# Finer groups of routing weights, exponents from one difference and two Relu, four more split units, and steps placed anew

## The reference, cut to what matters

```
x = x + attention(layernorm(x))                 # 8 sequences, 512 x 128
x = x + experts(layernorm(x))                   # first layer of experts
x = x + rwkv(layernorm(x))                      # time mixing, channel mixing
x = x + experts(layernorm(x))                   # second layer of experts

experts(x):                                     # 32 experts of width 64, top 4 of a softmax
    y = sum_e  w_e * ((silu(x @ W1[e]) * (x @ W3[e])) @ W2[e])
    z = (silu(x @ Ws1) * (x @ Ws3)) @ Ws2       # shared expert, width 128

wkv(w, u, k, v), for each token t, with carry aa, bb, pp:
    ww = u + k;   qq = max(pp, ww);   e1 = exp(pp - qq);   e2 = exp(ww - qq)
    y  = (e1 * aa + e2 * v) / (e1 * bb + e2)
    ww2 = pp + w; qq2 = max(ww2, k);  e1b = exp(ww2 - qq2); e2b = exp(k - qq2)
    aa, bb, pp = e1b * aa + e2b * v,  e1b * bb + e2b,  qq2
```

## Time and profile before

| | before |
|---|---|
| device time, median of 3 runs | 793.45 us |
| lowest and highest of the runs | 793.45 and 793.64 us |
| span of the profiled execution | 791.7 us |
| busy: PE / DVE / ACT / POOL | 99 / 82 / 72 / 79% of the span |
| DMA, mean over the span | 102 GB/s, 80.7 MB |

### The profile page before, as it was taken

One profiled execution on the slowest core, in us unless ns is written; L12 is line 12 of the kernel. 1 busy time (PEld: TensorE's weight loads), 2 busy tenths in 40 slices (PEclk: granted clock), 3 DMA queues, 4 the chain that ended last, 5 costly groups with the idle time before them and its releaser, 6 DMA issues.

```text
span 791.7 us, 12780 instructions
## 1 busy us (share of the span) xinstructions
PE 785.1 (99%) x3817; PEld 596.4 (75%) x3817; DVE 645.9 (82%) x1539; ACT 567.9 (72%) x1055; POOL 625.3 (79%) x491
## 2 busy tenths in 40 slices
PE   8999999999999999999999999999999999999998
PEld 5777778676776777768778777887778767788786
DVE  6875577997997989998988869988689889767686
ACT  5677787868768778689765867668685775677553
POOL 6687779849767797769987888998797877876985
PEclk9999999999999999999999999999999999999999
DMA  9353334243144342462425444253444424425552
GB/s 326 95 123 82 87 92 113 66 102 92 42 113 113 73 105 54 110 133 58 120 60 134 104 93 107 65 143 79 110 113 95 90 68 110 111 59 115 124 127 74
DMA packets 49332, 80.73 MB, mean 102 GB/s; under 512 B 3280, under 2 KB 14544, under 8 KB 48880
## 3 DMA queue, kind: packets, MB, share of 16 engines
q1 hardware_dynamic: 48976, 79.72, 42.1%
q10 hardware_dynamic: 288, 0.20, 0.1%
HBM read 75.19 MB, written 4.72 MB: 101 GB/s over the span
## 4 chain that ended last, share of the span: by engine, by line
PE 51%; POOL 2%; issue 2%; DVE 1%; ACT 0%; DVEq 0%; POOLq 0%; ACTq 0%
PE pa L1039 5%; PE pb L1039 4%; PE py L1067 4%; PE pa L1043 4%; PE pb L1043 4%; PE pa L1040 4%; PE pb L1040 4%; PE pu L1326 4%; PE py L1072 3%; PE py L1074 3%; PE py L1073 3%; POOL m_h L587 1%; PE pq L1283 1%; PE pu L1310 1%; PE pv L1334 1%
## 5 line engine op out<-in xcount | busy, mean ns | idle before, releaser
L587 POOL TENSOR_TENSOR m_h<-m_v,m_wb 128x512 f32<-128x512 f32 x254 | 364.3, 1444 | 98.7 <-DVE m_v L1468 42.9
L732 ACT ACTIVATE m_th<-pa 128x512 f32<-128x512 f32 x220 | 130.6, 594 | 102.0 <-PE pa L1043 97.7
L1468 DVE TENSOR_TENSOR m_v<-m_th,pb 128x512 f32<-128x512 f32 x205 | 138.6, 679 | 23.9 <-ACT m_th L732 15.5
L1039 PE MATMUL pa<-m_xh,w1h 128*128 128x512 f32 x272 | 137.2, 504 | 0.3 <-DVE m_v L1471 0.2
L416 DVE TENSOR_TENSOR m_hl<-m_h,m_hh 128x512 fp32r<-128x512 f32 x120 | 111.4, 929 | 24.8 <-ACT m_hh L921 24.1
L921 ACT ACTIVATE m_hh<-m_h 128x512 fp32r<-128x512 f32 x184 | 115.2, 626 | 13.8 <-POOL m_h L587 13.1
L1039 PE MATMUL pb<-m_xh,w3h 128*128 128x512 f32 x272 | 115.4, 424 | 0.0
L1043 PE MATMUL pa<-m_xl,w1h 128*128 128x512 f32 x272 | 107.3, 394 | 0.3 <-POOL m_xl L608 0.3
L1043 PE MATMUL pb<-m_xl,w3h 128*128 128x512 f32 x272 | 107.1, 394 | 0.0
L1040 PE MATMUL pa<-m_xh,w1l 128*128 128x512 f32 x272 | 106.6, 392 | 0.0
L1040 PE MATMUL pb<-m_xh,w3l 128*128 128x512 f32 x272 | 106.5, 391 | 0.0
(11 more groups left out here) (318 smaller groups left out, 1653.8 us busy)
## 6 DMA issues: line engine op xcount, KB each, us to landing
m_wb<-w_scratch SPq DMA_DIRECT2D x126, 512.0 KB, 6.5
x_sb<-in_x SPq DMA_DIRECT2D x8, 256.0 KB, 7.2
m_wb<-in_w SPq DMA_DIRECT2D x2, 1024.0 KB, 6.8
x_out<-x_sb SPq DMA_DIRECT2D x7, 256.0 KB, 6.6
u_scratch<-t_u SPq DMA_DIRECT2D x6, 256.0 KB, 2.6
t_u<-u_scratch SPq DMA_DIRECT2D x6, 256.0 KB, 2.7
f_kk<-in_w SPq DMA_DIRECT2D x1, 1024.0 KB, 9.7
w_scratch<-r_wT SPq DMA_DIRECT2D x16, 64.0 KB, 1.5
```

Of the source, the lines that this page charges most:

```text
L587: pool.tensor_tensor(hidden(g, p), gated(g, p), m_wb[:, p % (GRING * GP), :], ALU.mult).then_inc(sig["m_h"], 1)
L732: ins = act.activation(m_th[:, p % 2, :], pa[p % 2][:, :], ACT.Silu)
L1039: pe.matmul(ps[:, :], high[:, p, :], xh, start=True, stop=False)
L1468: dve.tensor_tensor(gated(g, p), m_th[:, r, :], pb[r][:, :], ALU.mult).then_inc(sig["m_v"], 1)
```

## The change

**Groups.** GROUPS goes from 4 to 8 and GRING from 2 to 4: a group is now two units, a load half as large, and a place of two units is loaded again as soon as these two are through. In pass 0 the first group is not loaded at all. The saved sequences' transfers (keep) are issued ahead of group 4 instead of group 2, that is, ahead of unit 8 in both.

**Time mixing.** `t_qq` on DVE and both differences on POOL go. DVE forms one difference for each pair, and ACT makes two Relu from it and then the Exp of the negative: four ACT instructions of 128 by 512 more for each sequence.

**Units.** Four units go from native to split (pass 0 unit 9, pass 1 unit 11, pass 4 unit 7, pass 13 unit 3), four more form `m_th` by Tanh (52 to 56), and the tables LOW_ON_POOL and LOW_LATE change: of the 188 rests 125 are on DVE and 63 on POOL, of the 184 before 120 and 64.

**Slots.** Nearly every table of slots has new numbers, on all five engines; the work in the steps is otherwise the same.

```diff
-GROUPS = 4
+GROUPS = 8
-GRING = 2
+GRING = 4
 NATIVE = (
-    (3, 9),
-    (11,),
+    (3,),
+    (),
...
+        def weights_in(g, j):
+            return 32 * (GROUPS // GRING * g + j // GRING + (0 if j % GRING == 0 else 1))
...
-                for j in range(GROUPS):
+                for j in range(1 if q == 0 else 0, GROUPS):
...
-                    first = SPREAD if q == 0 and j == 0 else 0
                     for h in range(2):
-                        sp.dma_start(m_wb[H * h:H * (h + 1), at + first:at + GP, :],
-                                     w_scratch[q, j, first:GP, h, :].partition_broadcast(H)).then_inc(wb_in[j], 16)
+                        sp.dma_start(m_wb[H * h:H * (h + 1), at:at + GP, :],
+                                     w_scratch[q, j, :, h, :].partition_broadcast(H)).then_inc(wb_in[j % GRING], 16)
...
-                if p % GP == 0 or (g == 0 and p == SPREAD):
-                    pool.wait_ge(wb_in[p // GP], 32 * g + 32)
+                if p % GP == 0:
+                    pool.wait_ge(wb_in[p // GP % GRING], weights_in(g, p // GP))
...
-                if slot == (26, 24, 24, 23, 25, 30, 32, 25)[m]:
-                    pool.wait_ge(sig["t_pp"], m + 1)
-                    pool.tensor_tensor(t_ea[:, 1, :], t_k[:, :], t_pp[:, 1:1 + S], ALU.subtract).then_inc(sig["t_a1"], 1)
-                if slot == (29, 29, 28, 29, 43, 32, 33, 30)[m]:
-                    pool.wait_ge(sig["t_qq"], m + 1)
-                    pool.tensor_tensor(t_eb[:, 0, :], t_pp[:, 0:S], maxima(m), ALU.subtract).then_inc(sig["t_b0"], 1)
...
                     act.wait_ge(sig["t_a0"], m + 1)
-                    act.wait_ge(sig["t_a1"], m + 1)
-                    act.activation(wide(t_ea[:, :, :]), wide(t_ea[:, :, :]), ACT.Exp).then_inc(sig["t_expa"], 1)
+                    act.activation(t_ea[:, 1, :], t_ea[:, 0, :], ACT.Relu).then_inc(sig["t_ra"], 1)
+                if slot == (29, 33, 33, 34, 38, 37, 33, 32)[m]:
+                    act.wait_ge(sig["t_ra"], 2 * m + 1)
+                    act.activation(t_ea[:, 0, :], t_ea[:, 0, :], ACT.Relu, scale=-1.0).then_inc(sig["t_ra"], 1)
...
+                if slot == (33, 35, 33, 34, 41, 38, 36, 32)[m]:
+                    act.wait_ge(sig["t_ra"], 2 * m + 2)
+                    act.activation(wide(t_ea[:, :, :]), wide(t_ea[:, :, :]), ACT.Exp, scale=-1.0).then_inc(sig["t_expa"], 1)
...
-                    dve.scalar_tensor_tensor(out=maxima(m), in0=t_k[:, :], scalar=vec[:, FIRST:FIRST + 1],
-                                             in1=t_pp[:, 0:S], op0=ALU.add, op1=ALU.max).then_inc(sig["t_qq"], 1)
-                if slot == (27, 29, 28, 29, 34, 39, 32, 29)[m]:
+                if slot == (27, 29, 28, 26, 35, 35, 26, 27)[m]:
                     dve.scalar_tensor_tensor(out=t_ea[:, 0, :], in0=t_pp[:, 0:S], scalar=decay[:, 0:1],
-                                             in1=t_pp[:, 1:1 + S], op0=ALU.add, op1=ALU.subtract).then_inc(sig["t_a0"], 1)
+                                             in1=t_k[:, :], op0=ALU.add, op1=ALU.subtract).then_inc(sig["t_a0"], 1)
...
```

371 lines of the change are left out of this document (186 added, 185 removed), and 4 rows, old and new, of the table NATIVE.

## The result

The changed kernel takes 795.69 us, the median of 20 runs (793.97 to 798.14), against 793.13 us of the kernel before (20 runs, 792.52 to 794.13): 2.6 us slower, and by the ratio of the runs 1.0029, 95% interval [1.0023, 1.0035]. The forecast was 793.8 us.

What follows compares the result with a forecast made beforehand. The prediction took TensorE, busy 99% of the span, to bound the kernel. From 793.45 us it added 1.8 for the start and took off 0.64 for split units and 0.8 for new places: 793.8 us, range 791.0 to 796.4.

Steps and rivals of the forecast that it cites:

- The start: Start of the kernel: sequence 1's statistics wait for its transfer, delaying row maxima and the router's transposes; +1.8 us, bounds 0 and 2.4.
- rival C: TensorE's clock falls in the new gap at the start, 1.6 us extra, 795.4 us; chance 0.10.
- Four split units: Four units turned from native to split save TensorE 0.16 us each, -0.64 us; what they add elsewhere costs nothing.
- TensorE's steps placed anew: TensorE's order: changes from small to fp32r matmuls fall from 156 to 147, 0.09 us each, -0.8 us.
- Time mixing and groups: Exponents by Relu on ScalarE and half-sized weight loads: both off TensorE's path, costed at nothing.
- the half pass between the exponents and their use: Time mixing: the cover that keeps its added ScalarE work free; without it, 0.63 us at each Relu ahead of a Silu.
- the forecast's case: Whole kernel: the forecast of 793.8 us, some 793.0 to 794.7; chance 0.42.
- slower: Whole kernel: a time above 795.04 us, told apart from no change by about 0.2%; chance 0.25.

## Why the prediction was right or wrong

**The start** (+1.8 us forecast). The mechanism is right step by step, up to the tenth. Its size was 1.7 us against the execution profiled before, and is nearer 1.2 against others, since the earlier trace rows come from an execution whose matmuls went at the full rate early. The term was taken from one execution, and that moment moves the old start by 0.2 to 1.0 us from trace to trace, which the bounds of 0 and 2.4 cover but the working doesn't name. What I had not seen is that two causes give the same end: with the maxima early again, GpSimd's order and a root stretched by 0.9 us hold `r_q` at 21.87.

**The clock** (rival C, given 0.10). By the granted clock of the executions it happens in 11 of 20, and costs 1.9 us where it does (796.34 - 794.41; 1.6 forecast). What was wrong is the weight: I argued that fillings on both sides protect the gap, and with the same fillings around it the clock fell in 11 of 20. With the gap filled it fell in none of 11. Its length alone doesn't decide either: with transposes at 15.40 behind an idle 2.28 us it fell in four of five (statistics ahead of everything), and behind an idle 2.33 us it stayed up in the profiled execution of the native units. What does decide is open. That C's 795.4 is so near the measured median is in part luck: it stands on a sum of 793.8, and the executions without the fall have 794.4.

**Four split units** (-0.64 us). Right for TensorE's work, 0.7 us. The statement that what they add costs nothing elsewhere is right only in the new order, where taking them back costs 0.8 to 1.0 us; alone in the old one they bring waits of about 1.8 us.

**TensorE's steps placed anew** (-0.8 us). Wrong, and wrong as a reading of the profile. I took the 0.32 us between the first and the second fp32r matmul behind small ones for 0.09 us of a price per change of kind. Look at the small matmul ahead of it instead, in the trace of the kernel before:

```profile
99.80 0.27 PE L1224 MATMUL pq<-ident,r_p 128*128 128x128 f32 x1
99.83 0.48 PE L1039 MATMUL pa<-m_xh,w1h 128*128 128x512 f32 x1
100.15 0.40 PE L1040 MATMUL pa<-m_xh,w1l 128*128 128x512 f32 x1
```

The small product starts at 99.80 and the next matmul 0.03 us behind it, though a small one takes TensorE 0.11 us (the three transposes from 309.85 to the next row at 310.18 take 0.33). The 0.09 us behind it are the small one's own time, which shows one interval late: from the fp32r matmul ahead (99.57) to the second one behind (100.15) are 0.58 us, and without a small one between them it is twice 0.23, 0.46 us; the difference is 0.12 us, the small one's own time. Fewer changes of kind don't remove it.

What the new places do instead isn't settled. I add up over each order the usual start-to-start time of each matmul, the median over all traces of the same matmul in the same surroundings, from the first L1039 of pass 0 to the last of pass 15. With one neighbour on each side as the surroundings this gives 753.8 us both before and after, with two ahead and one behind 754.6 and 753.7. The split units alone give 0.7 less in either count. So the new places lie between a cost of 0.6 us and a gain of 0.3 us of work; the 0.8 us are not in either.

**The middle as a whole.** From the first to the last of these matmuls (24.17 to 783.17 before, 25.88 to 784.26 after; the first of after stands above). Before:

```profile
24.17 0.48 PE L1039 MATMUL pa<-m_xh,w1h 128*128 128x512 f32 x1
```

```profile
783.17 0.40 PE L1039 MATMUL pb<-m_xh,w3h 128*128 128x512 f32 x1
```

After:

```profile
784.26 0.39 PE L1042 MATMUL pb<-m_xh,w3h 128*128 128x512 f32 x1
```

The stretch takes 759.0 us before and 758.4 after. But two experiments whose middle is that of the kernel before take 757.9 and 758.4, and five with the middle of the change 758.1 to 758.6. So on the mean the middle has gained 0.1 us, not the forecast 1.4, and the traces of the old order alone are 1.1 us apart. Since the split units do give 0.7, the rest of the middle has lost about as much. Which part of it did is open: no run has the tanh units, the tables LOW_ON_POOL and LOW_LATE, or the slots of the middle alone.

**Time mixing and groups** (nothing each). Right for the groups, alone and together. For time mixing nearly right as placed in the change, where one wait of 0.3 us stands behind the exponents' longest stretch on ScalarE, and wrong by 19 us in the old order. I named the wrong cover ("the half pass between the exponents and their use"): what the rows of both orders point to is how long these operations keep ScalarE from the Silu or Tanh of the next unit.

**The sum.** 793.8 was forecast from +1.8 - 0.64 - 0.8. In executions with the clock up it is about +1.2 for the start and about 0 for the middle, 1.3 measured; half of the executions add 1.9, and the median lies between, at +2.6. The sign is as forecast, though the forecast had it only as the small difference of a real term and one that isn't there. The size was too small by the term that double-counted a matmul's time and by a rival that I had held for unlikely. By the prediction's own limits 795.69 us is not the forecast's case (793.0 to 794.7) but above 795.04, "slower", which had 0.25; it is inside the full range, 791.0 to 796.4.

## What to carry to other kernels

A step moved to the front is only as early as the data that it reads: look up the landing of its transfer, and move the transfer with it. A start-to-start distance that looks like a price of what follows may be the time of what stands ahead, shown late; compare the pair, and an isolated case, before multiplying it by a count. And where one engine bounds a kernel at 99%, a new idle stretch of 2 us at the start can cost twice, once as idle time and once as a fallen clock, in some executions only; one profile doesn't show it, and here eight matmuls without use in the gap made it go.

## What the runs showed of the hardware

- VectorE and GpSimd hold each other up by whole operations on SBUF. GpSimd's inverse root took 1.93 us beside a rounding of 1.22 us and 1.02 alone; four fp32 scalings on VectorE took 3.05 us beside GpSimd's subtractions and 1.11 alone; two took 1.51 and 0.47. The page "SBUF — State Buffer" of the Trainium skill (section SBUF: two separate sides) calls the port pair that the two share an exclusive lock, held for the whole instruction; these rows agree. It means that an "idle" stretch of GpSimd isn't free for work if VectorE's chain beside it is the one that is waited for.
- The granted clock fell to the lower level behind TensorE's idle stretch of about 2 us in some executions and not in others of one and the same kernel (11 of 20 by the mean clock). In the trace that has it, it is 0.53 from 16 to 19 us and 1.00 from 19 us on. In the run with time mixing alone it fell in mid-kernel, behind waits of 0.88 and 1.80 us: 0.52 from 475.0 to 478.5 us.
- The same transfer of 256 KB takes 8.2 us behind two of 1 MB and 4.1 us ahead of them (median of two).
- The moment from which the first matmuls go at the full rate differs between executions, from 4.9 us in the trace of before to 7.6 us in that of time mixing alone, and moves the old start by 0.2 to 1.0 us. The profile's granted clock doesn't show it: it reads 1.00 from 1 us on in the traces of before and after, while the first eight matmuls take 3.40 and 3.59 us.
